# Routed experts of a two-block transformer layer: casts of the row numbers on another engine, the scaling of gathered rows and the turn of the gated rows at other places of their queues

## The reference, cut to what matters

```python
def _moe(x, Wgate, expert_bias, Wg, Wu, Wd, sWg, sWu, sWd):      # E = 8 experts, K = 2 for each row, I = 256
    xf = x.reshape(-1, c)                                          # 4096 rows of 512
    shared = jnp.mean(_experts(xf, sWg, sWu, sWd), axis=1)
    probs = jax.nn.softmax(xf @ Wgate + expert_bias, axis=-1)
    topk_p, topk_i = jax.lax.top_k(probs, K)
    topk_p = topk_p / jnp.sum(topk_p, axis=-1, keepdims=True)
    comb = jnp.sum(jax.nn.one_hot(topk_i, E, dtype=xf.dtype) * topk_p[..., None], axis=1)
    routed = jnp.einsum('ne,nec->nc', comb, _experts(xf, Wg, Wu, Wd))   # silu(x Wg) * (x Wu), then Wd
    return (shared + routed).reshape(b, t, c)
```

## Time and profile before

| | us |
|---|---|
| median of 3 runs | 2520.12 (2515.02 to 2522.04) |
| the profiled execution, its own time | 2519.39 |
| its span, first to last instruction | 2517.6 |
| routed part, first gather to the end of the span | 2098.0 to 2517.6 |
| start of the first addition, of the last | 2116.9, 2511.1 |

### The profile page before, as it was taken

One profiled execution on the slowest core, in us unless ns is written; L12 is line 12 of the kernel. 1 busy time (PEld: TensorE's weight loads), 2 busy tenths in 40 slices (PEclk: granted clock), 3 DMA queues, 4 the chain that ended last, 5 costly groups with the idle time before them and its releaser, 6 DMA issues. The chain is left out here.

```text
span 2517.6 us, 50422 instructions
## 1 busy us (share of the span) xinstructions
PE 2193.4 (87%) x12864; PEld 977.5 (39%) x12865; DVE 1510.5 (60%) x4072; ACT 1200.9 (48%) x2316; POOL 1403.5 (56%) x1598
## 2 busy tenths in 40 slices
PE   3699999999999854999999999999858875888887
PEld 1233333343333212444444444444334432444443
DVE  4578888887888824665555655555337672333332
ACT  3255555555555423454554545545445542444443
POOL 3167777676767641455555555555614564555554
PEclk9899999999999976999999999999979887999999
DMA  4413223233232113344442434424135554555554
GB/s 156 147 49 108 96 88 110 70 109 99 85 106 77 55 67 118 116 143 119 128 133 90 142 119 127 144 90 124 58 131 118 143 118 73 94 95 95 92 92 79
DMA packets 221402, 264.60 MB, mean 105 GB/s; under 512 B 37400, under 2 KB 163468, under 8 KB 220852
## 3 DMA queue, kind: packets, MB, share of 16 engines
q1 hardware_dynamic: 197628, 212.81, 27.5%
q0 software_dynamic: 22976, 48.38, 11.1%
q10 hardware_dynamic: 520, 0.27, 0.0%
HBM read 162.12 MB, written 86.80 MB: 99 GB/s over the span
## 5 line engine op out<-in xcount | busy, mean ns | idle before, releaser
L464 ACT ACTIVATE a_pt<-a_bank 128x512 f32<-128x512 f32 x512 | 305.1, 597 | 362.0 <-DVE a_bank L567 351.7
L1345 DVE CUSTOM_DVE_ANT_0 b_bank<-b_bank,b_tri 128x256 f32<-128x256 f32 (+3 forms) x512 | 253.7, 498 | 322.6 <-PE b_bank L1483 313.6
L578 DVE CUSTOM_DVE_ANT_0 a_bank<-a_bank,a_strip 128x512 f32<-128x512 f32 x512 | 354.4, 693 | 20.5 <-PE a_bank L721 17.9
L1130 POOL TENSOR_TENSOR b_acc<-b_acc,b_pt 128x256 f32<-128x256 f32 (+2 forms) x384 | 271.7, 725 | 105.7 <-ACT b_pt L1219 84.3
L374 POOL TENSOR_TENSOR a_acc<-a_acc,a_pt 128x512 f32<-128x512 f32 x256 | 317.7, 1270 | 11.7 <-ACT a_pt L464 8.3
L567 DVE TENSOR_TENSOR a_bank<-a_bank,a_band 128x256 f32<-128x256 f32 (+1 forms) x512 | 205.5, 402 | 132.1 <-PE a_bank L708 130.3
L1219 ACT ACTIVATE b_pt<-b_bank 128x256 f32<-128x256 f32 (+2 forms) x384 | 143.4, 381 | 203.4 <-PE b_bank L1467 194.7
L721 PE MATMUL a_bank<-a_k_stack,a_q_stack 97*128 97x512 f16 x512 | 197.0, 385 | 17.3 <-DMA a_k_stack<-mask_rows 10.2
L708 PE MATMUL a_bank<-a_q_stack,a_k_stack 128*128 128x512 f16 x512 | 197.6, 388 | 15.3 <-ACT a_pt L464 10.5
L1800 POOL DMA_INDIRECT out_dram<-c_z,c_to_row x72 | 115.1, 1598 | 141.0 <-DMA out_dram<-c_z,c_to_row 114.9
L2174 DVE SCALAR_TENSOR_TENSOR c_hid<-c_th,c_bank 128x256 f32<-128x256 f32 x72 | 30.3, 421 | 229.1 <-ACT c_th L1937 229.1
(11 more groups left out here) (337 smaller groups left out, 5628.1 us busy)
## 6 DMA issues: line engine op xcount, KB each, us to landing
b_q_stack<-qk_rows SPq DMA_DIRECT2D x192, 128.0 KB, 2.7
a_q_stack<-qk_rows SPq DMA_DIRECT2D x96, 128.0 KB
a_k_stack<-qk_rows SPq DMA_DIRECT2D x96, 128.0 KB
b_k_stack<-qk_rows SPq DMA_DIRECT2D x96, 128.0 KB, 2.7
a_xn<-in_x SPq DMA_DIRECT2D x32, 256.0 KB, 2.7
a_cn<-in_ctx SPq DMA_DIRECT2D x32, 256.0 KB, 2.9
qk_rows<-a_qk_hi SPq DMA_DIRECT2D x64, 128.0 KB, 1.7
qk_rows<-a_qk_lo SPq DMA_DIRECT2D x64, 128.0 KB, 1.8
```

The lines of the kernel that those rows point to most:

```text
L464: nc.scalar.activation(pt[:, n % SLOTS, :], st_bank[n % 2][:], ACT.Exp).then_inc(exped, 1)
L578: nc.vector.tensor_tensor_reduce(out=max_bank[step % 2][:], in0=max_bank[step % 2][:], in1=strip[:, g * HG + hh, at:at + S], scale=-1.0, s ...
L1130: nc.gpsimd.tensor_tensor(sums_of, sums_of, probs(n), ALU.add).then_inc(pooled, 1)
L1345: nc.vector.tensor_tensor_reduce(out=max_bank[step % 2][:, 0:w], in0=max_bank[step % 2][:, 0:w], in1=tri[:, at:at + w], scale=-1.0, scalar ...
```

## The change

On POOL both casts go away; on DVE they come in, `set_from_row` for block j+4 behind the low half of rows, `set_to_row` for block j at the end of the step, and `set_from_row` of blocks 0 to 3 ahead of the loop. `set_to_row` waits for the landing of the addition four blocks earlier. On ACT the scaling of rows j+2 moves ahead of `h_hi` of j-1, and `y_out` waits for `to_set` in place of `from_set`. On PE the turn of gated rows j-1 moves from ahead of the twelve up products of j to behind the third of them.

```diff
 def gather(at):
-    pool.wait_ge(entered[u], at.use * 16 + 32)
+    pool.wait_ge(from_set, j + 1)
     if not at.within(0, 3):
         pool.wait_ge(x_turned, j + (AHEAD - 3))
     pool.nop(nofuse=True)
-    nc.gpsimd.tensor_copy(from_row[:, u, :], entry[:, bass.ds(j, 1), 0]).then_inc(from_set, 1)
-    pool.wait_ge(from_set, j + 1)
-    pool.nop(nofuse=True)
     pool.indirect_dma_start(x_in[:, u], None, z_all, ...).then_inc(gathered[u], 16)
 def scatter_add(at):
-    nc.gpsimd.tensor_copy(to_row[:, u, :], entry[:, bass.ds(j, 1), 1]).then_inc(to_set, 1)
     pool.wait_ge(to_set, j + 1)
...
 # ACT, step j
     x_high(j + 1, u + 1)
+    scale_rows(at.back(-2))
     act.wait_ge(x_hid_turned, j + AHEAD)
     act.wait_ge(x_down, j + (AHEAD - 2))
     nc.scalar.activation(hidden_rows(h_hi, u + 1), ...)
-    scale_rows(at.back(-2))
...
-    act.wait_ge(from_set, j + 3)
+    act.wait_ge(to_set, j)
...
 # DVE
+def set_from_row(at):
+    dve.wait_ge(entered[at.slot], at.use * 16 + 32)
+    v.tensor_copy(from_row[:, at.slot, :], entry[:, bass.ds(at.n, 1), 0]).then_inc(from_set, 1)
+def set_to_row(at):
+    if not at.within(0, 3):
+        dve.wait_ge(added[at.slot % 2], at.use * 32 + (at.slot // 2 * 16 - 16))
+    v.tensor_copy(to_row[:, at.slot, :], entry[:, bass.ds(at.n, 1), 1]).then_inc(to_set, 1)
...
 # PE, x_up_to: inside the loop over k
     last = mm(up_bank[w][:], xt_lo[:, w, k, 0:P], weights(gu_hi), start=False, stop=(k == NK - 1))
+    if k == 0 and not at.within(0, 0):
+        turn_hidden(at.back(1).n, u + 1)
```

More of the change, by code:

```diff
@@ L1811, in step @@
                     scatter_add(at.back(2))
-                if at.within(NB - 3, NB):
-                    pool.sem_inc(from_set, 1)
-                else:
+                if not at.within(NB - 3, NB):
                     gather(at.back(-3))
@@ L1927, in step @@
                     x_high(j + 1, u + 1)
+                if not at.within(NB - 2, NB):
+                    scale_rows(at.back(-2))
                 if not at.within(0, 0):
@@ L1931, in step @@
                     nc.scalar.activation(hidden_rows(h_hi, u + 1), hid_bank[(u + 1) % 2][:, 0:I], ACT.Copy).then_inc(x_h_hi, 1)
-                if not at.within(NB - 2, NB):
-                    scale_rows(at.back(-2))
                 if not at.within(NB, NB):
@@ L2158, in x_low @@
                                 ALU.subtract).then_inc(x_lo_done, 1)
+            def set_from_row(at):
[5 more added lines that the diff above has]
+                v.tensor_copy(to_row[:, at.slot, :], entry[:, bass.ds(at.n, 1), 1]).then_inc(to_set, 1)
+            for j in range(4):
+                set_from_row(Count(0, j, 4))
             def step(at):
@@ L2165, in step @@
                     x_low(j + 1, u + 1)
+                if not at.within(NB - 4, NB):
+                    set_from_row(at.back(-4))
                 if not at.within(0, 0):
@@ L2178, in step @@
                                            op0=ALU.mult, op1=ALU.mult).then_inc(x_hidden, 1)
+                    set_to_row(at)
             over(dve, step)
@@ L2281, in x_turn, with x_up_to @@
                 last.then_inc(x_turned, 1)
-            def x_up_to(j, u, e):
-                w = u % 2
+            def x_up_to(at, e):
+                j, u, w = at.n, at.slot, at.slot % 2
                 pe.wait_ge(x_lo_done, j + (AHEAD + 1))
@@ L2334, in step @@
                     x_turn(x_in[:, after.slot], after.n, after.slot)
-                if not at.within(0, 0):
+                if at.within(NB, NB):
                     turn_hidden(at.back(1).n, u + 1)
-                if not at.within(NB, NB):
-                    x_up_to(j, u, own)
+                else:
+                    x_up_to(at, own)
                 if not at.within(0, 0):
```

## The result

The changed kernel takes 2551.55 us (median of 4 runs, 2546.72 to 2554.23), the kernel before, run beside it, 2519.04 (2515.02 to 2522.04): ratio 1.0118, 95% interval 1.0099 to 1.0137. It is slower by 32 us, where I had +4 as the likeliest and 2542 as the upper end. The profiled execution took 2554.23 us with a span of 2552.3. Of all the runs reported here, one execution of ten with the turn alone was a slow one, 3273.35 us at a granted clock of 0.65; it is left out of that run's ratio.

What follows compares the result with a forecast made beforehand. The prediction took POOL's own serial cycle as the bound before the change; 50 steps x (5.56 + 0.07 - 5.55) = +4.0, 14 steps +0, start -1, end +1 gave 2523.4, as median 2524 us; range 2505 to 2542.

Steps and rivals of the forecast that it cites:

- gather to scaling: From POOL's gather to ACT's scaling: 3.51 to 3.92 us, the upper value taken because the DMA engines are busy.
- two-block loop: `y_out` through addition, gather, scaling, `h_hi`, `h_lo` and down products back to `y_out`: 11.11 us, 5.56 a step.
- rival 3: The gather queues behind the addition on the DMA engines: 2544 us in full, 2533 likeliest; chance 0.28.
- fourteen landing steps: Steps whose addition on POOL waits for the previous addition's landing: 5.68 us each, unchanged, +0.
- Casts off POOL: On POOL, the gap between addition and gather shrinks from 0.99 to 0.30; POOL's own cycle becomes 4.44, no longer the bound.
- Casts on DVE: Two casts a step on DVE at 0.17 us each, holding up nobody who isn't waiting anyway: 0.
- Rival 4: DVE's casts wait while POOL writes descriptors, holding `h_lo` by up to 1.60 us: +53, 2573 us; chance 0.05.
- The turn inside the up products: On PE, three up products cover the 0.52 us wait for gated rows: 0 in the ordinary step.
- PE sets no step: In the routed part PE has 50 us to spare, so freeing PE time does not shorten a step.
- Rivals 1: A shorter loop, with gap 0 and 3.51 from gather to scaling: 5.20 us a step, -14, 2506 us; chance 0.21.
- Rival 2: Gathers land so early that no one waits and PE bounds the step at 4.86 us: -31, 2489 us; chance 0.05.

Runs made afterwards that it cites:

- the trace with everything: The changed kernel with the scaling behind `h_hi`, the gather issued ahead of the addition and PE's lookups where they are used: 2453.62 us, ratio 0.9736.

## Why the prediction was wrong

The mechanism was right and its size was off. The step that failed is the gather's landing: the prediction took 3.92 from gather to scaling, and 4.44 was measured. Term by term, the two-block loop as the prediction had it, and as the changed kernel has it on the mean of blocks 2 to 65 (distances between starts in the timelines of POOL, ACT, DVE and PE; the first is from the end of `y_out`):

| link | predicted | measured |
|---|---|---|
| `y_out` to its addition | 1.54 | 1.67 |
| addition to gather | 1.90 | 1.89 |
| gather to scaling | 3.92 | 4.44 |
| scaling to `h_hi` | 0.63 | 0.65 |
| `h_hi` to `h_lo` | 0.45 | 0.40 |
| `h_lo` to the first down product | 0.48 | 0.66 |
| down products to `y_out` | 1.50 | 1.66 |
| `y_out` | 0.69 | 0.69 |
| sum | 11.11 | 12.06 |

The measured links follow each other from one addition to the second behind it, so their sum, 6.03 a step, must be the interval (6.02 between additions 2 and 66); it proves nothing by itself. That this loop sets the step is shown by the runs: a link shortened by 0.62 took 0.34 off each interval, and opening the loop at either of two places (the scaling back, the gather first) took over 60 us away. What the table shows is which links were taken too short. Against 5.58 before, 64 steps make +28 us of the 31 between first and last addition: the 50 ordinary ones went from 5.54 to 6.01, where 5.63 was forecast.

- **Gather to scaling** is the term that failed, 0.52 of the 0.95. The prediction took 3.92 because "issued earlier it finds them busy", the upper of two rows. But those rows had the gather 2.6 us behind the addition; moved up by 0.7 it landed 0.1 sooner, so the term had to grow by most of the 0.7. This was rival 3, whose full value was 6.51 from addition to scaling; 6.33 was measured. The prediction had the mechanism and its sign, over 4.1 from gather to scaling, and still gave it 0.28. Its range ended at 2542, although this rival at its full value came to 2544.
- **Three small latencies** are most of the rest: 0.13, 0.18 and 0.16. For the down products to `y_out` I used the first block, which runs outside the hardware loop; inside it this link is 1.62 in most steps of the kernel before too, so that the right value could have been read there. That the difference is register work inside the loop is an inference; the 0.15 of issue between L2177 and L2322 in the chain above is one such piece.
- **The fourteen landing steps** were kept at 5.68 as steps of their own. With ordinary steps at 6.01 they are 6.07, from 5.72 before: all 64 pay, and these fourteen pay 5 us that the sum had at 0.
- **Casts off POOL**: right. The gap fell from 0.99 to 0.30 and POOL stopped being the bound. POOL's own cycle without casts was put at 4.44; 3.18 is what the trace with everything shows, which changes nothing here. The run with the casts alone gives their worth, 24 us, which the prediction had not seen at all, since it only ever priced them together with the moved scaling.
- **Casts on DVE**: right, 0. A cast takes 0.14 us, whatever POOL does (duration ns min/median/max, first and last start):

```profile
L2156 DVE CAST c_from_row<-c_entry x72: 143/144/154, 2101.0 to 2511.8; 128x1 int32 x64, 128x1 int32<-128x1 f32 x8
```

  None of the 72 takes longer than 0.154, and 59 of them run while POOL is in a DMA instruction; one of these had idle time of DVE ahead of it, 0.86 for its entries from the table. Rival 4 is out. The Trainium skill's rule that a VectorE cast in a two-port mode and GpSimd lock each other out ("SBUF — State Buffer", section "Who interferes with whom") does not reach a cast of one element a partition, as far as this trace shows.
- **The turn inside the up products**: right, 0 in the kernel before.
- **"PE sets no step"**: right, though its wait ahead of the down products laid open 1 to 1.5 us of lookups that I had not looked for. They cost 4 us in the changed kernel.
- Rivals 1 and 2 did not occur in the changed kernel. Rival 2 did in the run with the gather first, the scaling back and the lookups at their use, at 4.58 a step and not 4.86: the prediction's 0.32 and 0.64 for the two turns are 0.22 and 0.44 there, and the twelve and six products are 2.60 and 1.30 as it had them.

The Trainium skill's rule on ring order ("DMA: Bandwidth & Descriptors", section "Queues, rings and completion order") would let the gather move forward by less than POOL saves; the traces agree, with 6.42 from addition to scaling before and 6.33 after.

## What to carry to other kernels

Before an instruction is moved ahead of another on an in-order engine, ask what it waits for and follow that wait round until it comes back: here one scaling put a gather, and through POOL's queue the previous `y_out`, ahead of `h_hi`, at 31 us; the same place costs nothing once the gathers are issued first and PE's lookups are moved to their use. A latency read between two transfers on one queue can be a property of their distance: here the second, pulled 0.7 us closer, took 0.64 us longer, so price the sum from the first, not the second alone. Ask also what is exposed once the bound is gone: the lookups were worth 4 us inside the loop and 35 us once it was open. And price the parts of a change one by one as well as together: two of the three parts here gain 35 us, and with the gather first and the lookups at their use the kernel takes 2453 us, 68 less than the kernel before beside it, with PE busy 99% of the middle of the routed part.

## What the runs showed that I had not expected

- Lookups on PE's queue (`value_load`) are hidden while PE has matmuls in hand: with them at their use and the gathers early PE is idle for 0.1 us of 290. Behind a wait of PE they showed as up to 1.53 us of "issue" in the changed kernel. Moved to their use they gave back 4, 10, 35 and -13 us in four orders of the other work.
- POOL starts one indirect DMA 0.30 us behind another even with waits on semaphores between them, as long as these are already met.
- One read of a register value on POOL, 0.29 us and its arithmetic, was worth 22 us of the whole kernel, because it stood in the loop.
